# Issuing the half copies of the payload one run of scatters ahead, in the first stage of a mixture-of-experts kernel

## The reference

```
x = x + 0.5 * ffn(layernorm(x))
x = x + attention(layernorm(x))
x = x + 0.5 * ffn(layernorm(x))

ffn(x):  scores = x @ router                      # 8 experts
         top 2 of 8 per token, gate = sigmoid(score)
         y_e = (silu(g*x @ w_in[e]) * (g*x @ w_sw[e])) @ w_out[e]
         shared = silu(x @ w_in_sh.T) * (x @ w_sw_sh.T) @ w_out_sh.T
         return shared + sum of y_e over the chosen experts
```

## Time and profile before

| | us |
|---|---|
| Three runs | 982.34, 975.77, 981.61 |
| Median of the runs | 981.61 |
| Time of the profiled execution | 974.14 |
| Span of the profiled execution | 972.40 |
| First stage, to the landing of its scatters | about 0 to 210 |
| First expert stage | 214 to about 408 |
| Attention stage | about 410 to 700 |
| Second expert stage and last sums | about 703 to 972 |

### The profile page before, as it was taken

The page is one execution under the profiler, slowest core; times in us unless marked ns, Lnnn a source line. Parts: engine busy times, 40 slices in busy tenths (PEclk is TensorE's granted clock), DMA queues, the critical chain, the costliest instruction groups (busy, mean ns, idle before and its releaser), DMA issues. The chain is left out here.

```text
span 972.4 us, 19487 instructions
## 1 busy us (share of the span) xinstructions
PE 828.4 (85%) x5857; PEld 725.8 (75%) x5857; DVE 641.4 (66%) x2022; ACT 572.9 (59%) x1662; POOL 643.2 (66%) x701
## 2 busy tenths in 40 slices
PE   4787677609999999559999999997589999998997
PEld 3676566509999999525777677776489999997786
DVE  6786655506666666237899999886456666664665
ACT  3324132106777777369888888872167777775332
POOL 4777777745777777571488887677547777776331
PEclk9898778858999999869999999998689999999999
DMA  9611111322333333151022111111433333331763
GB/s 242 187 45 47 45 45 44 89 60 70 108 104 106 108 104 106 49 165 53 25 72 81 59 56 43 37 42 39 84 90 106 107 103 105 106 107 63 222 194 102
DMA packets 112920, 88.01 MB, mean 91 GB/s; under 512 B 13426, under 2 KB 102132, under 8 KB 112820
## 3 DMA queue, kind: packets, MB, share of 16 engines
q1 hardware_dynamic: 94816, 51.08, 20.5%
q0 software_dynamic: 17280, 35.69, 10.9%
q10 hardware_dynamic: 724, 0.01, 0.0%
HBM read 43.68 MB, written 43.04 MB: 89 GB/s over the span
## 5 line engine op out<-in xcount | busy, mean ns | idle before, releaser
L867 POOL DMA_INDIRECT results<-YO,XS x284 | 275.6, 970 | 120.1 <-issue 85.1
L846 DVE TENSOR_TENSOR HT<-bank,SG 128x512 f32<-128x512 f32 x142 | 98.2, 691 | 132.6 <-PE bank L941 132.5
L939 PE MATMUL bank<-XSH,WX 128*128 128x256 f32 x568 | 174.0, 306 | 0.3 <-DVE WX L855 0.3
L1047 POOL DMA_INDIRECT pairs<-PAY,POS x128 | 134.3, 1049 | 59.0 <-issue 28.8
L411 POOL DMA_INDIRECT pairs<-PAY,POS x128 | 126.3, 987 | 57.8 <-issue 30.8
L940 PE MATMUL bank<-XSL,WX 128*128 128x256 f32 x568 | 162.1, 285 | 0.0
L941 PE MATMUL bank<-XSH,WX 128*128 128x256 f32 x568 | 161.8, 285 | 0.0
L957 PE MATMUL bank<-WOE,HT 128*128 x1136 | 150.3, 275 | 0.1
L957 PEld LDWEIGHTS bank<-WOE,HT 128*128 128x128 f32 x1136 | 138.1, 192 | 0.5 <-issue 0.5
L895 ACT ACTIVATE XG<-XS 128x128 f32<-128x128 f32 x284 | 111.1, 392 | 43.3 <-DMA XS<-pairs 43.3
L914 ACT ACTIVATE SG<-bank 128x512 f32<-128x512 f32 x142 | 84.9, 598 | 48.5 <-PE bank L941 48.4
(11 more groups left out here) (197 smaller groups left out, 1742.6 us busy)
## 6 DMA issues: line engine op xcount, KB each, us to landing
XS<-pairs SPq DMA_DIRECT2D x142, 130.0 KB
Y<-results SPq DMA_DIRECT2D x32, 256.0 KB, 3.2
YF<-results SPq DMA_DIRECT2D x32, 256.0 KB, 4.0
results<-YO,XS POOLq DMA_INDIRECT x284
pairs<-PAY,POS POOLq DMA_INDIRECT x256, 2.3
out<-X SPq DMA_DIRECT2D x16, 256.0 KB, 2.8
pairs<-pad_rows SPq DMA_DIRECT2D x16, 130.0 KB, 4.1
pairs<-pad_rows SPq DMA_DIRECT2D x1, 1040.0 KB, 15.7
```

Of the source, the lines that this page charges most:

```text
L846: dve.tensor_tensor(HT[:, i % 2, :], bank[4 + i % 2][:, :], SG[:, i % 2, :], ALU.mult)\
L867: pool.indirect_dma_start(results, bass.IndirectOffsetOnAxis(ap=XS[:, u, j, AT_DEST:AT_DEST + 1].bitcast(U32), axis=0), YO[:, u, j, :], No ...
L939: pe.matmul(ps, WX[:, i % 2, 1, w], hi, start=True, stop=False)
L1047: pool.indirect_dma_start(pairs, bass.IndirectOffsetOnAxis(ap=POS[:, b % AB, j, c:c + 1], axis=0), PAY[:, b % AB, c, j, :], None).then_inc ...
```

## The change

The copy and the four scatters of a half become two functions, `second(b, h)` and `scatter(b, h)`, and GpSimd's queue is written in another order: each copy stands in front of the run of four scatters that comes before its own. The instructions, their sizes, and the semaphores are the same.

```diff
+                def second(b, h):
+                    half = slice(h * BT // 2, (h + 1) * BT // 2)
+                    if h == 0:
+                        pool.wait_ge(k["normed"], b + 1)
+                    pool.tensor_copy(PAY[:, b % RB, 1, half, 0:D], PAY[:, b % RB, 0, half, 0:D]).then_inc(k["pay1"], 1)
+
+                def scatter(b, h):
+                    if h == 0:
+                        pool.wait_ge(k["gated"], b + 1)
+                        pool.wait_ge(k["placed"], b + 1)
+                    pool.wait_ge(k["pay1"], 2 * b + h + 1)
+                    for j in range(h * BT // 2, (h + 1) * BT // 2):
+                        for c in range(TOPK):
+                            pool.indirect_dma_start(
...
+                second(0, 0)
                 for b in range(NB):
-                    for h in range(2):
...
+                    second(b, 1)
+                    scatter(b, 0)
+                    if b + 1 < NB:
+                        second(b + 1, 0)
+                    scatter(b, 1)
                     if b == 1:
```

More of the change, by code:

```diff
@@ L397, in _ @@
                 st.did(pool.tensor_copy(tile_no[:, :], tile_i[:, :]))
-                for b in range(NB):
-                    for h in range(2):
[L401 to L413, removed]
+                def second(b, h):
[11 more added lines that the diff above has]
+                            pool.indirect_dma_start(
+                                pairs, bass.IndirectOffsetOnAxis(ap=POS[:, b % RB, j, c:c + 1], axis=0),
+                                PAY[:, b % RB, c, j, :], None).then_inc(scattered1[b % RB], 16)
+                second(0, 0)
+                for b in range(NB):
+                    second(b, 1)
[3 more added lines that the diff above has]
+                    scatter(b, 1)
                     if b == 1:
```

## The result

The changed kernel took 966.73 us in the median of four runs, the kernel before 978.69 us in four runs beside it: a ratio of 0.9877 with the interval 0.9834 to 0.9921. It is faster by 1.2%. (One run of the four, 981.61 us, was disturbed and is not part of the ratio.) The profiled executions are 966.89 us (span 965.1) and 974.14 us, 7.25 us apart.

What follows compares the result with a forecast made beforehand. POOL's queue was taken to set the first stage's end; 0 (starts) + 1.65 (middles) + 0.38 (last middle) = 2.0 us less, 981.61 - 2.0 = 979.6 us. Range 971.5 to 984, its lower end using 4.2 us for the middles.

Steps and rivals of the forecast that it cites:

- the gap of 0.81 us: Between copy and scatter at a block's start: put down to `gated` and `placed`, expected to stay, gain 15 x 0 us.
- The two rows that I read as a chain of waits: Starts in the first block and attention stage: copy long done, scatter 0.94 and 0.77 us after `POS` was written.
- Rival A: Whole gap was the wait for the copy: start and middle both fall to 0.17, 11.6 us saved, 970.0 us; chance 5%.
- The gap of 0.28 us: Between copy and scatter in a block's middle: falls to 0.17 us, 15 x 0.11 = 1.65 us saved.
- The row with the addition: POOL addition of 1.27 us between scatters, not waited for; next scatter 0.17 us later, taken as the middle's new gap.
- B: Rival: short copy hides too little, middle gap stays 0.28 to 0.30 us, only the last middle gains; 981.3 us; chance 30%.
- The last middle: Middle of the last block loses its copy: 0.40 and 0.28 us become a gap of 0.30, 0.38 us saved.
- The wait that moves: Wait for `normed` before the next block's first copy, now in the middle of the block before: cost none.
- The copies' own length: POOL's copies, most 0.41 us, some 0.75 beside DVE's subtraction: left at their present cost.
- C: Rival: copies at starts and middles meet DVE's subtraction (L527), 0.35 us each; 6.1 us slower, 987.7 us; chance 5%.
- The idle time of 1.84 us: Single long gap inside the first stage's scatter runs: left as it was; a second one would cost 1.5 us.
- no later stage can take the gain back: After the first stage: all engines begin again together and nothing reaches over its end, so POOL's saving arrives whole.

Runs made afterwards that it cites:

- e14: Changed kernel, but the first half's scatters wait for the newest copy, right in front of them: 979.49 us, 0.9963 of the kernel before.
- e11: Changed kernel, but the second half's scatters wait for the newest copy: 1056.11 us in one run, beside 1055.60 for the kernel before.
- e1: Changed kernel again, no edit, on chips where the kernel before takes some 1,054 us: 1071.18 us, 1.0155 of the kernel before.
- e5: Changed kernel once more, no edit, on chips where the kernel before takes some 1,054 us: 1065.72 us, 1.0099 of the kernel before.
- e18: Changed kernel, but DVE's subtraction reads PSUM in place of SBUF and PE's next turn waits for it: 979.77 us, 0.9995 of the kernel before.
- e15: Kernel before, its order kept, but the waits for `gated` and `placed` moved ahead of the first half's copy: 967.06 us, 0.9864 of the kernel before.
- e16: Against the changed kernel, ACT makes the copies and POOL's queue keeps the scatters alone: 953.85 us, 0.9742 of the kernel before.
- e2: Changed kernel, first half's scatters waiting for the newest copy, where the kernel before takes some 1,054 us: 1054.83 us, 1.0004 of the kernel before.
- e10: Against the kernel before, both copies of a block stand in front of its first scatter, none in the middle: 1058.87 us, 1.003 of it.
- e3: Kernel before with `gated` and `placed` waits ahead of the first half's copy, where it takes some 1,054 us: 1061.39 us, 1.0067 of it.
- e12: Changed kernel, DVE's subtraction reading PSUM, PE's next turn waiting, where the kernel before takes some 1,054 us: 1074.62 us, 1.017 of the kernel before.
- e6: Changed kernel, first half's scatters waiting for the newest copy, repeated where the kernel before takes some 1,054 us: 1058.13 us, 1.0038 of it.
- e4: Against the changed kernel, ACT makes the copies, where the kernel before takes some 1,054 us: 1081.45 us, 1.0247 of the kernel before.
- e13: Changed kernel again, no edit, on chips where the kernel before takes 981 to 984 us: 971.04 us, 0.9886 of the kernel before.
- e17: Changed kernel, with the new order for the attention stage's last three blocks too: 963.45 us, 0.9848 of the kernel before.
- e8: Changed kernel, new order also in the attention stage's last three blocks, where the kernel before takes some 1,054 us: 1068.89 us, 1.0136 of it.
- e9: The kernel before once more, no edit, for its trace on chips where it takes some 1,054 us: 1050.10 us in one run.

## Why the prediction was wrong, step by step

**"I cost this gap at no gain: 15 x 0 us."** This is the step that failed, and it alone carries the miss: the gap of 0.81 us was worth 0.64 at each of 15 starts, 9.6 us. The two rows that I read as a chain of waits with a finished copy do show one, but in both the last of the waits, `placed`, was *not met* when the queue came to it. They show what it costs to be held at that instruction, 0.77 to 0.94 us, by whatever semaphore. I took it for what it costs to stand behind such waits. In the 15 other starts `placed` was met: `POS` was written 2.9 to 24 us before the block's first scatter. For the scatter at 161.49 DVE's timeline has it 17.4 us before:

```profile
143.87 0.22 DVE L239 TENSOR_REDUCE POS<-PICK 128x8 uint32<-128x64 f32 x1
```

What was not met there was the copy, and e14 shows that this alone makes the 0.81 us. (The 0.043 us of L408 can't tell the two apart: the record is as short where a copy held the queue. And this instruction, which I took for one of the further waits, carries the wait for `pay1` too.) Met waits cost nothing, which the earlier trace rows showed and I used for the middle only.

Rival A was right in what happened (both gaps 0.17, 11.6 us) and had 5%. What I held against it was the same misreading. That its 11.6 us also come near the 12.0 between the medians is in part luck: four terms that it did not have, +1.5, +2.3, -5.2 and -0.1 us, left 10.2 at the stage's end.

**The gap of 0.28 us, taken to 0.17.** Right: 0.16 to 0.17 in the changed kernel, and e11 has both values side by side. The row with the addition was the right one; the shorter copy hides as much. B, with 30%, fell.

**The last middle**, 0.38 us: right. The added copy lies in front, 8.50 to 9.24 us, and the first scatter began at 19.34, 0.11 later, with `POS`.

**The wait that moves**, at no cost: right here. Of the middle copies none waited for `normed`. DVE waits for landed scatters 16.7 us in five waits in place of 27.0 in six. What I did not ask was who else must keep up when POOL is faster: `placed` had no cost in my account, and its lateness took much of the gain in e1, e5 and e18.

**The copies' own length**, left as it was; and **C**. The contention was real but moved the other way. Copies over 0.6 us went from seven to one. Scatters over 1.1 us went from 7 to 17. I had priced only what a copy can lose beside L527, since scatters of 0.97 us stood everywhere; but the earlier trace rows's own 1.15 us and the trace's six others were there to be asked about. The Trainium skill, SBUF — State Buffer, section "SBUF: two separate sides", says that a VectorE operation with two SBUF inputs locks out a GpSimd operation that reads SBUF, for a whole instruction. The row of 160.38 agrees, if a scatter, which reads its row numbers from SBUF, counts as such an operation: 0.59 us were left of the subtraction, and the scatter took 0.48 longer.

**The idle time of 1.84 us**, left alone: wrong by 1.5 us, to the good. It shows only where the queue was held shortly before (last section), so it went with the held starts.

**The sum and the median.** 2.0 us were forecast, 10.3 came at the stage's end. A stage later the saving was still 9.9 us, so "no later stage can take the gain back" held that far; at the end of the two traces it is 7.3, and whether the change has a part in that loss is not shown. The range's lower end, 971.5, was set by 4.2 us for the middles and nothing for the starts; had A had the chance that its arithmetic deserved, the range would have reached it.

## What to carry to other kernels

A gap after a wait is to be read by which wait was unmet when the queue got there: a row in which *another* wait ended last prices being held, not the waits in general. Where the wait for an instruction just issued can't be avoided, the cheapest form is the one that the waiting instruction carries itself, behind all waits that are met early (e15), and cheaper still is work in between (the change) or another engine for the work (e16). When the engine that sets the end gets faster, ask of each semaphore it waits for how far ahead its producer is; the same edit gave 1.2% here and cost 1.0 to 1.6% where the producers were late.

## What the runs showed of the hardware

- **Three prices for one wait** on GpSimd's queue, before an indirect DMA and behind a short copy: 0.17 us if it was met, 0.28 if the DMA carries it and is held, 0.81 if the queue's own wait instruction is held. In the last case the DMA begins 0.73 us after the end of that instruction, in the kernel before, in e2, e10 and e14 alike (0.89 in the first block), and also where `placed` held it (e1, e18).
- **The queue runs ahead of the engine.** In the changed kernel the line's records between 20 and 50 us (count, shortest, median and longest ns, first and last start) are

```profile
L409 POOLq EVENT_SEMAPHORE  x3: 43/782/3404, 24.8 to 47.5; - x3
```

  The one of 3.40 us begins at 24.80, while POOL has still to execute four scatters (24.93 to 29.70) and a copy that come before it in the program. `placed` came 3.4 us after the queue asked for it, and no scatter was late for that: the next began at 30.27, with its gap of 0.17. The Trainium skill, Perfetto Trace Analysis, GPSIMD Engine Instruction, has the sequencer ready for the next instruction once it has pushed one into the wait queue, where the semaphores are awaited; the row agrees, with five instructions pushed and not yet executed.
- **A gap tied to a place in the program.** The 1.84 us stand before the 114th scatter of the first stage in the kernel before, in e2, e3, e5 to e12, e14 and e18, at 188.4 to 215.4 us (1.48 in e6). The attention stage has one of about 2.0 before its own 114th. The first is gone in the change, e1, e4, e13, e16 and e17, and 0.41 in e15; the second in e17 alone, though e8 has the same order there. It is a stall of the queue, and the engine doesn't notice it when the queue is ahead: counted from the end of the queue's own wait before the 113th scatter, the 114th begins 3.56 us later in twelve of the thirteen (3.91 in e3; in e6 the 113th itself took longer, which leaves 1.48), and where the gap is gone that wait had ended 4.4 us before (e1) or more. In the attention stage it is 3.74 us, in e8 too, where a late `placed` held POOL, and 3.77 in e17, where POOL had other scatters to execute in that time. What the queue does in that time was not shown.
- **The lock reaches indirect DMAs.** A scatter that begins with 0.25 us left of a subtraction of two SBUF operands takes 1.09 us in place of 0.97, with 0.60 us left 1.46 (both in e13). With one of the operands in PSUM (e12, e18) none beside it is over 1.1 us.
- **Chips on which the same program waits longer.** Where the kernel before takes 1,054 us, ACT and DVE wait for what the profile calls remote, in the first stage (see e9) and in the first expert stage, there at line 900 ten times and for 12.5 us in all; in the kernel before and after of the result they do not (waits of ACT in e9):

```profile
ACT XSH L900 <- remote: 12.5, 10, 2.5
```

  The granted clock hardly shows it: 0.97 in the first expert stage of e1, 0.99 in that of the kernel after. Why the orders that hold POOL least lose most there, though the first stage of the kernel before is no longer than elsewhere, stays open: no run told what the remote waits are, and that it is TensorE's results that come late is read from who waits (ACT and DVE, for its banks).
